# Order of the three product passes and place of one wait in a fused cross-attention kernel

## What is computed

```
x = x + tanh(g_xattn) * xattn(layernorm(x), ctx)      # 16 heads of 64, 1444 context rows of 96
x = x + tanh(g_ffn)   * ffn(layernorm(x))             # rmsnorm, self-attention of 16 heads of 8,
                                                      # top-2 of 8 experts and a shared one
# xattn, per head:
sim  = (x w_q) (ctx w_k)^T / 8
attn = softmax(sim)
out  = attn (ctx w_v);  then  out w_o + b_o
```

## Time and profile before

| | |
|---|---|
| median of 3 runs | 1496.37 us (1490.59 to 1496.73) |
| profiled execution, its own time | 1497.34 us |
| its span | 1495.6 us |
| TensorE (PE) busy | 1362.4 us, 91% |
| VectorE (DVE) busy | 1058.8 us, 71% |
| ScalarE (ACT) busy | 809.3 us, 54% |
| GpSimd (POOL) busy | 589.5 us, 39% |
| mean granted clock of TensorE | 0.975 |

### The profile page before, as it was taken

How to read it: one execution, slowest core, us unless ns; L and a number is a source line. 1 busy time by engine, 2 the same in 40 slices (tenths; PEclk the granted TensorE clock), 3 DMA queues, 4 the chain that set the end, 5 groups by cost and what they waited for, 6 DMA issues and landing times.

```text
span 1495.6 us, 23587 instructions
## 1 busy us (share of the span) xinstructions
PE 1362.4 (91%) x8776; PEld 826.5 (55%) x8776; DVE 1058.8 (71%) x1996; ACT 809.3 (54%) x1188; POOL 589.5 (39%) x702
## 2 busy tenths in 40 slices
PE   4759999999999999999999999999999999788898
PEld 4235555555656565655555555555555555456676
DVE  2677677767686767676777777777777775866765
ACT  1034656555655655555556565656565655554654
POOL 3023334343443444443444343434343433453554
PEclk9589999999999999999999999999999999999999
DMA  7020202020201001020202020202020100000000
GB/s 218 29 57 1 58 1 58 1 58 1 58 1 37 23 21 38 2 57 1 58 1 58 1 58 1 58 1 58 1 57 2 43 1 1 1 1 2 7 7 11
DMA packets 66934, 42.86 MB, mean 29 GB/s; under 512 B 52966, under 2 KB 62410, under 8 KB 66826
## 3 DMA queue, kind: packets, MB, share of 16 engines
q1 hardware_dynamic: 66826, 41.43, 10.7%
HBM read 15.38 MB, written 0.82 MB: 11 GB/s over the span
## 4 chain that ended last, share of the span: by engine, by line
PE 66%; DVE 14%; POOL 9%; issue 4%; ACT 4%; DMA 2%; SPq 0%; DVEq 0%; POOLq 0%; ACTq 0%
PE psum L755 19%; PE psum L815 8%; PE psum L736 7%; PE psum L738 7%; PE psum L740 7%; DVE mx L1239 4%; POOL p_lo L431 4%; PE psum L768 4%; PE psum L855 3%; PE psum L807 3%; PE psum L842 3%; PE psum L781 3%; PE psum L864 2%; DVE p_lo L431 2%; DVE y_sb L1261 2%
## 5 line engine op out<-in xcount | busy, mean ns | idle before, releaser
L950 ACT ACTIVATE p<-psum 128x800 f32<-128x800 f32 x384 | 320.9, 836 | 522.9 <-PE psum L740 521.0
L1239 DVE TENSOR_REDUCE mx<-psum 128x1 f32<-128x512 f32 (+1 forms) x624 | 385.8, 653 | 63.4 <-PE psum L815 58.0
L431 POOL TENSOR_TENSOR p_lo<-p,p_hi 128x800 f16<-128x800 f32 x128 | 243.9, 1906 | 468.3 <-ACT p_hi L951 461.8
L755 PE MATMUL psum<-p_hi,c_both 128*128 128x400 f16 x1536 | 389.3, 335 | 25.0 <-POOL p_lo L431 14.3
L951 ACT ACTIVATE p_hi<-psum 128x800 f16<-128x800 f32 x384 | 319.3, 831 | 0.0
L815 PE MATMUL psum<-cT_both,qk_hi 96*128 96x512 f16 (+1 forms) x624 | 231.1, 387 | 54.5 <-DVE y_sb L1261 16.4
L431 DVE TENSOR_TENSOR p_lo<-p,p_hi 128x800 f16<-128x800 f32 x256 | 259.4, 1013 | 21.4 <-ACT p_hi L951 18.9
L755 PEld LDWEIGHTS psum<-p_hi,c_both 128*128 128x128 f16 x1536 | 146.7, 98 | 145.5 <-issue 33.7
L736 PE MATMUL psum<-qk_hi,cT_both 97*128 97x400 f16 x768 | 195.5, 335 | 2.9 <-DMA qk_hi<-mrow 2.9
L755 PE MATMUL psum<-p_lo,c_both 128*128 128x400 f16 x768 | 194.6, 335 | 0.0
L738 PE MATMUL psum<-qk_lo,cT_both 96*128 96x400 f16 x768 | 194.5, 334 | 0.0
(11 more groups left out here) (183 smaller groups left out, 1795.7 us busy)
## 6 DMA issues: line engine op xcount, KB each, us to landing
c_both<-c_new SPq DMA_DIRECT2D x16, 768.0 KB, 4.9
ctx_nat<-in_ctx_dram SPq DMA_DIRECT2D x16, 528.0 KB
wg<-in_L_ffn_e_gate_dram SPq DMA_DIRECT2D x1, 1024.0 KB, 5.5
wu<-in_L_ffn_e_up_dram SPq DMA_DIRECT2D x1, 1024.0 KB, 7.5
wd<-in_L_ffn_e_down_dram SPq DMA_DIRECT2D x8, 128.0 KB, 4.9
out_dram<-x SPq DMA_DIRECT2D x4, 200.0 KB
x<-in_x_dram SPq DMA_DIRECT2D x1, 600.0 KB
p<-in_L_xattn_w_q_dram SPq DMA_DIRECT2D x1, 512.0 KB, 4.1
```

Source lines behind the costliest of these rows:

```text
L431: engine.tensor_tensor(p_lo[0:m, i % 3, :, :], p32[0:m, i % 3, :, :], p_hi[0:m, i % 3, :, :], ALU.subtract).then_inc(lo_made(b, i)[0], 1)
L755: t = mm(outs[k], w[parity][0:m, j, :], p[0:m, i % 3, k, :], start=(j == 0 and w is c_hi and p is p_hi), stop=(j == CH - 1 and w is c_lo))
L950: a(p32[0:m, i % 3, :, :], src, ACT.Exp, scale=DH ** -0.5)
L1239: v.tensor_reduce(mx[:, rt, part:part + 1], bank[:, 0:w], AX.X, ALU.max)\
```

## The change

In `pv_unit` the wait for `p_lo` moves from the front of the unit to a place inside it. The order of the passes was (context high, probability high), (context high, probability low), (context low, probability high); it becomes (context high, probability high), (context low, probability high), (context high, probability low). The wait stands in front of the last pass. The side work of the middle third stays behind the first pass. For units 22 and 23 of the last batch, which no score unit precedes, a wait for `probs_hi` is put ahead.

```diff
                 j = i % CH
                 m = kc(j)[1]
-                pe.wait_ge(*lo_made(b, i))
                 if i == 0:
                     pe.wait_ge(c_in, (b + 1) * 16)
                 if j == 0 and not (isinstance(b, int) and b == 0 and i == 0):
                     pe.wait_ge(acc_out, b * 2 + i // CH)
                 outs = [psum[:, ACCB + k, 0:GW] for k in range(2)]
-                for w, p in ((c_hi, p_hi), (c_hi, p_lo), (c_lo, p_hi)):
+                for n, (w, p) in enumerate(((c_hi, p_hi), (c_lo, p_hi), (c_hi, p_lo))):
+                    if p is p_lo:
+                        pe.wait_ge(*lo_made(b, i))
                     for k in range(2):
                         t = mm(outs[k], w[parity][0:m, j, :], p[0:m, i % 3, k, :],
-                               start=(j == 0 and w is c_hi and p is p_hi), stop=(j == CH - 1 and w is c_lo))
-                    if w is c_hi and p is p_hi:
+                               start=(j == 0 and n == 0), stop=(j == CH - 1 and p is p_lo))
+                    if n == 0:
                         between()
                 t.then_inc(pv, 1)
...
             for i in (UNITS - 2, UNITS - 1):
+                pe.wait_ge(probs_hi, (B - 1) * UNITS + (i + 1))
                 pv_unit(B - 1, 1, i)
```

## The result

| | kernel before | changed kernel |
|---|---|---|
| median of 16 runs, us | 1492.63 (1490.19 to 1497.68) | 1496.51 (1494.67 to 1500.80) |
| profiled execution, us | 1497.34 | 1497.40 |
| its span, us | 1495.6 | 1495.7 |

The account below looks back on a forecast made before the run. TensorE was taken to set the pace in most places, its stalls counting only if nothing else is late. Terms 0 + 0 + 0 + 0 - 1.03 + 0 = -1.0 us, from the 1496.37 us median: 1495.4 us, range 1489.5 to 1499.5.

Parts of the forecast that it names:

- Order of the passes: In all 384 units: six matmuls before and after, same operands, each loading its weights anyway; 0 us.
- The old wait in the middle batches: Unit 6: first pass starts 0.80 us earlier, but the transposition behind it still waits for `hn`; 14 x 0 us saved.
- First batch: Unit 0: TensorE is 0.68 us early, then stands for the transfer of the next batch's context; 0 us saved.
- Last batch, unit 6: TensorE is free at 1277.46, but the transposition stands behind `hn` until 1283.02; 0 us saved.
- Last batch, unit 9: TensorE leaves about 1.2 us earlier, but VectorE's `p_lo` of unit 11 sets the pace; 0 us, bound 1.2 us.
- Units 18 to 23: Last batch: four matmuls go ahead of the wait and unit 23's last pass starts earlier; 1.03 us saved at stage end.
- The rest of the program hangs on that end: After the last batch: sums copy, output matrix and last norm follow its end, so the 1.03 us reaches the total.
- The wait in its new place: Between fourth and fifth matmul of 384 units: a passed wait costs 0, with 3.8 us of resolution either way.
- the first (the stalls come back in full): Rival: `hn` or VectorE do not hold the engine, or come earlier; 14.2 us saved, 1482.2 us; chance 0.06.
- the second (the moved wait costs): Rival: the wait breaks the dense matmul row, 0.05 us in each of 384 units, 1514.6 us; chance 0.02.
- The third: Rival: one 5.2 us stall in the last batch prolongs the low clock; 5.3 us more, 1500.7 us; chance 0.07.
- the base: Whole kernel: the median of the three runs shown, 1496.37 us, from which the forecast of 1495.4 us was taken.

Follow-up runs that it names:

- e2: Changed kernel with the wait for `p_lo` back in front of the unit in all batches, so the new order alone; 1492.51 us, ratio 1.0008.
- e4: Changed kernel with the wait moved only in the last batch, in front of the unit in the first 15; 1496.35 us, ratio 1.0027.
- e5: Changed kernel with the old wait in front again in unit 6 of the last batch alone; 1495.09 us, ratio 1.0005.
- e6: Changed kernel with the old wait in front again in units 18 to 23 of the last batch alone; 1492.52 us, ratio 0.9991.
- e7: Changed kernel with the wait moved only in units 18 to 23 of the last batch, old wait everywhere else; 1496.28 us, ratio 1.0008.
- e11: Changed kernel with the 32 small matmuls split into 16 and 16, one expert unit between them; 1492.30 us, ratio 0.9995.
- e14: Changed kernel with two expert units moved so that the small matmuls stand in rows of 8, 16 and 8; 1493.73 us, ratio 1.0000.
- e15: Changed kernel with both expert units moved between two halves of 16 small matmuls; 1493.65 us, ratio 1.0007.
- e9: Changed kernel with two extra ScalarE copies ahead of its second copy of the sums, to delay the expert stage; 1500.15 us, ratio 1.0030.
- e12: Kernel before with the small matmuls split into 16 and 16, one expert unit between them; 1493.76 us, ratio 0.9992.
- e8: The changed kernel again, unaltered, for a second profile; 1495.40 us, ratio 1.0008.
- e13: The changed kernel once more, unaltered, on the same chip as the two later splits; 1496.22 us, ratio 1.0009.
- e3: Changed kernel with the old wait in front of the unit in the last batch alone; 1494.29 us, ratio 1.0012.
- e10: Changed kernel with one extra ScalarE copy ahead of its second copy of the sums; 1496.35 us, ratio 1.0005.

## Why the prediction was wrong

Point by point, by its own steps:

- **Order of the passes: 0.** Held: e2 to e4 show no cost in their medians that stands clear of their intervals.
- **The old wait in the middle batches: 14 x 0.** Held. The transposition waits for `hn`, 0.75 us of idle time in the batch shown, and starts where it did (the prediction had 655.69 to 656.59, 0.90 us, of which the tail of the first pass counts as busy). Over the 14 batches the two profiles keep their distance to within 0.05 us, and a middle batch takes 77.66 to 77.68 us in both wherever nothing else differs.
- **First batch: 0, the 0.68 us taken back.** Held: the wait for the context has grown from 9.84 us to 10.56, by 0.72 us.
- **Last batch, unit 6: 0.** Held (1282.75 for 1283.02 at an offset of 0.27).
- **Last batch, unit 9: 0, with a bound of 1.2 us.** Held: 1.28 us early there, and none of it left in VectorE's `p_lo` of unit 11.
- **Units 18 to 23: -1.03 us at the end of the stage.** Held, and a little more: 1.18 us. VectorE's last `p_lo` runs at 1332.42, which with the offset is 0.49 us ahead of its old 1333.18; the forecast had 0.33.
- **"The rest of the program hangs on that end."** This is the step that failed. I passed the 1.03 us on to the end without looking at what the expert stage does when it starts earlier, and put the term of its clock at 0. It measures +1.6 us where the clock falls once, and +4.5 to +4.7 us where it falls a second time (the table). -1.2 + 1.6 is 0.4 us for an execution like the one profiled, and a loss of some 3.4 us where the clock falls twice; the medians of the first comparison say +3.9 us, which is a little beyond both. The chain from the copy on was in the profile of before, with the 32 small matmuls in it, and I did not read it, since no line of it is in the diff.
- **The wait in its new place: 0.** Held: 0.34 us from pair to pair with the passed wait between them.

Of the rivals, the first (the stalls come back in full) and the second (the moved wait costs) are refuted by the same rows. The third was right in its kind, a stretch of low clock as the price of the change, and wrong in its place: the clock behind the one long stall of the last batch is no worse than it was (0.50 over 1281.6 to 1288.4 us for 1281.9 to 1288.7), and e5 and e6 show that this stall has nothing to do with it. The price came 90 us later.

A second mistake is in the base. I took the median of three runs (1496.37 us), 6 us apart, as what the kernel takes; over 16 runs it is 1492.63. The forecast of 1495.4 us was near the measured 1496.51 because two errors, of 3.7 us in the base and 4.9 us in the effect, go against each other. As a change of time it was wrong.

**What is shown and what isn't.** Shown: each local step above; that the stage of the experts is 1.5 us or more longer in all six profiles of the table with the moved end and nothing put in; that the moved waits of units 18 to 23 alone do this (e7, one profile, 1 of 11 runs below 1493 us) and all others together don't (e6, one profile, 7 of 12 runs); that the fall at that place is gone when the row of 32 small matmuls is broken up (e11, e14 and e15, one profile each). Not settled: the size. The first comparison gave 1.0025, the two repeats 1.0008 and 1.0009 with intervals that hold 1, on chips where the kernel before was itself slower; a loss is clear of its interval in the first comparison alone. Also open is why the clock falls when the small matmuls start 2.1 us or more ahead of that fixed moment and not when they start 2.0 us ahead; e9, whose delay made a low stretch of its own, could not tell. No version tried beats the kernel before clear of its interval; the nearest are e6 (0.9991) and e12 (0.9992).

## What to carry to other kernels

Before a saving at the end of one stage is passed on to the end of the program, read the granted clock of the next stage as well, above all behind rows of very small matmuls: a shift of 1 us there can cost more than it gave. A stall of TensorE is worth nothing if the instruction behind the matmuls it frees waits for something else longer still; here that was so 15 times out of 16, and in 14 of them it was longer by only 0.1 us. When an effect is a quarter of a per cent, three runs are no base; and a stage's length, measured from one row to the end in several profiles, tells what medians don't. A kernel whose runs lie in bunches is better compared by how many runs fall into each.

## What the runs showed of the hardware that I had not expected

**A TensorE that the profile shows as busy can lose its clock.** In the changed kernel the engine is shown as busy for 3.00 of 3.00 us over 1371 to 1374, with the 32 fp32 matmuls of 9 columns and what follows them, and the clock is 0.50 over 1374 to 1377. The same happened in seven of the first twelve profiles of the table, at that place. When the 32 are split (e11, e14, e15), it does not fall there. The busy share says little about the work in such a row: the 32 start 0.09 us apart (2.7 us from the first to the last) and have 9 columns each, where matmuls of 400 columns start 0.17 us apart.
The Trainium skill (TensorE: Matmul & The Clock Gate, "HAM oscillation — how this bites in real kernels") explains falls of this kind by an idle TensorE between bursts. The second place agrees so far as idle time stands there: 1.84 us in e4 until 1391.03, with the clock at 0.50 from 1391.2 on. The same stall is in the kernel before (1.84 us until 1395.08) and no fall comes with it. The first place has no idle time in the rows, and there the traces go beyond that section.

**What a low stretch costs:** 3.4 us at 0.50 cost 1.6 us of the stage (changed, e7, e8), and 10.2 us in two stretches cost 4.5 to 4.7 (e2, e4, e5, e13). That is nearly half of their length: the other engines (VectorE is busy for 96.19 of 146 us in e3) hide little of it.

**A stall of 2.42 us can do the same.** In e9 TensorE stands for 2.42 us ahead of 1336.41, and the clock is 0.54 over 1336 to 1339. The other profiles have a stall of 1.02 us at this place, e10 one of 1.72 us, and none has a low clock there. It is one profile.

**Passed waits inside a row of matmuls** cost nothing that the rows resolve, also in the middle of a product unit: 0.34 us from pair to pair. In the changed profile 374 of the 384 last passes start 0.17 us behind the matmul ahead of them, which is the step of dense matmuls.
